# Gathers of the score stage: a wait for V's first half before each group's first gather

## The reference

```python
h = jnp.maximum(_layernorm(x, axis=-1), 0.0)
Q, K, V = ((h @ W).reshape(n, H, D) for W in (Wq, Wk, Wv))      # H = 8 heads of D = 32
scores = jnp.einsum('ehd,ehd->eh', Q[dst], K[src]) * SCALE
# softmax of the scores over the edges of one dst, w
msg = V[src] * w[:, :, None]
out = jnp.zeros((n, H, D), msg.dtype).at[dst].add(msg)
# then: output projection, residual, layer norm, feed-forward with gelu, residual, layer norm
```

## Time and profile before

| what | value |
|---|---|
| median of three runs (lowest to highest) | 1763.69 us (1762.94 to 1768.16) |
| the profiled execution | 1771.17 us |
| its span, first to last instruction | 1769.3 us |
| busy: PE, DVE, ACT, POOL | 93%, 86%, 75%, 72% of the span |
| score stage | from the start to about 402 us |

### The profile page before, as it was taken

The page is one execution under the profiler, slowest core; times in us unless marked ns, Lnnn a source line. Parts: engine busy times, 40 slices in busy tenths (PEclk is TensorE's granted clock), DMA queues, the critical chain, the costliest instruction groups (busy, mean ns, idle before and its releaser), DMA issues.

```text
span 1769.3 us, 31077 instructions
## 1 busy us (share of the span) xinstructions
PE 1642.7 (93%) x10389; PEld 1472.7 (83%) x10389; DVE 1512.9 (86%) x4615; ACT 1320.0 (75%) x2419; POOL 1270.5 (72%) x1281
## 2 busy tenths in 40 slices
PE   2878888799888999999999999999999999999997
PEld 2767777687666899999999999999999999999997
DVE  1566666778773899999999999999999999999997
ACT  1465556565444888888888888888888888888884
POOL 7364545505666788888888888888888888888883
PEclk7798889999988999999999999999999999999999
DMA  5487637713425577777777777777777777777761
GB/s 173 142 311 269 239 131 274 288 37 127 133 100 125 123 171 179 176 170 177 177 171 176 175 174 176 175 175 172 176 176 174 174 178 172 175 178 172 174 138 66
DMA packets 95280, 303.91 MB, mean 172 GB/s; under 512 B 16236, under 2 KB 21834, under 8 KB 95120
## 3 DMA queue, kind: packets, MB, share of 16 engines
q0 software_dynamic: 42336, 138.54, 38.9%
q1 hardware_dynamic: 52784, 163.38, 26.5%
HBM read 134.61 MB, written 118.53 MB: 143 GB/s over the span
## 4 chain that ended last, share of the span: by engine, by line
PE 84%; issue 6%; DVE 4%; ACT 3%; another core or an unknown queue 2%; DMA 0%; DVEq 0%; SPq 0%; POOLq 0%; POOL 0%; ACTq 0%
PE banks L962 32%; PE banks L951 30%; PE banks L384 8%; PE banks L937 5%; PE banks L406 3%; PE banks L904 2%; PE banks L392 2%; ACT a_hs L335 2%; DVE c_total L811 1%; PE banks L923 1%; PE banks L376 1%; DVE c_msg L799 1%; ACT a_htd_hi L302 1%; PE banks L893 0%
## 5 line engine op out<-in xcount | busy, mean ns | idle before, releaser
L962 PE MATMUL banks<-d_w_hi,d_act_hi 128*128 128x256 f32 x1564 | 457.4, 292 | 0.0
L962 PE MATMUL banks<-d_w_lo,d_act_hi 128*128 128x256 f32 x1564 | 442.0, 283 | 0.0
L962 PE MATMUL banks<-d_w_hi,d_act_lo 128*128 128x256 f32 x1564 | 441.6, 282 | 0.0
L1159 ACT ACTIVATE vt<-vt,d_zx_nmr,d_zx_rstd 128x256 f32<-128x256 f32 x391 | 222.8, 594 | 141.6 <-POOL d_zx_nmr L1278 141.6
L951 PE MATMUL banks<-d_zt_hi,d_w_hi 128*128 128x512 f32 (+1 forms) x784 | 306.8, 391 | 2.2 <-DVE d_zt_lo L1044 2.2
L951 PE MATMUL banks<-d_zt_lo,d_w_hi 128*128 128x512 f32 (+1 forms) x784 | 306.4, 391 | 0.0
L951 PE MATMUL banks<-d_zt_hi,d_w_lo 128*128 128x512 f32 (+1 forms) x784 | 305.4, 390 | 0.0
L962 PEld LDWEIGHTS banks<-d_w_hi,d_act_lo 128*128 128x128 f32 x1564 | 298.9, 191 | 0.0
L962 PEld LDWEIGHTS banks<-d_w_hi,d_act_hi 128*128 128x128 f32 x1564 | 298.5, 191 | 0.0
L962 PEld LDWEIGHTS banks<-d_w_lo,d_act_hi 128*128 128x128 f32 x1564 | 297.9, 190 | 0.0
L1260 POOL TENSOR_TENSOR vt<-vt,d_g_row 128x1024 f32<-128x1024 f32 x98 | 289.3, 2952 | 2.9 <-ACT vt L1159 2.9
(11 more groups left out here) (167 smaller groups left out, 3629.4 us busy)
## 6 DMA issues: line engine op xcount, KB each, us to landing
agg_scratch<-vt SPq DMA_DIRECT2D x100, 512.0 KB
vt<-in_x SPq DMA_DIRECT2D x97, 512.0 KB
vt<-agg_scratch POOLq DMA_DIRECT2D x97, 512.0 KB, 5.5
vt<-vt POOLq DMA_DIRECT2D x97, 512.0 KB, 7.5
out<-vt SPq DMA_DIRECT2D x97, 512.0 KB, 2.9
a_xd<-in_x,a_idx POOLq DMA_INDIRECT x98
a_xs<-in_x,a_idx POOLq DMA_INDIRECT x98
score_scratch<-a_score SPq DMA_DIRECT2D x98, 4.0 KB
```

Source lines behind the costliest of these rows:

```text
L962: ins = nc.tensor.matmul(Y[s % 2][:, j, :], a[:, c, j * P:(j + 1) * P], w[:, c, :], start=False, stop=(c == KF - 1 and w is w2_lo), skip_g ...
L1159: ins = nc.scalar.activation(zn[gz % 2][:, j, :], z[gz % ZR][:, j, :], ACT.Identity, bias=zx_nmr[:, at % NR, 0, j:j + 1], scale=zx_rstd[:, ...
```

## The change

GpSimd waits once more before the first gather of each group from group 4 on, for the first half of V of step g - 4:

```diff
@@ -166,6 +166,8 @@
                         continue
                     if g >= XG and j == 0:
                         pool.wait_ge(h_done[side], g + 1 - XG)
+                    if g >= XG + 1 and n == 0:
+                        pool.wait_ge(v_done, KD * (g - XG - 1) + 1)
                     at = g * 2 * GT + n
                     nc.gpsimd.indirect_dma_start(
                         xg[side][g % XG][:, j, :], None, x, bass.IndirectOffsetOnAxis(idx[:, at:at + 1], 0),
```

## The result

The changed kernel took 1799.45 us (median of five runs, 1798.23 to 1804.04) against 1763.69 us of the kernel before (now over five runs, 1758.46 to 1768.16): a ratio of 1.0208, 95% interval 1.0182 to 1.0234. It is slower by 35.8 us in the medians; the forecast was +38. The profiled execution took 1799.45 us with a span of 1797.6 us, 28.3 us more than the span in the profile before.

The account below looks back on a forecast made before the run. Gather bursts hold back TensorE's completions in the score stage; one burst of eight over Q and K makes steps 16.8 us, so 20 x (16.8 - 14.91) = +38, 1763.7 + 38 = 1802 us; own range 1768 to 1820, 8-in-10 range 1731 to 1822.

Parts of the forecast that it names:

- Lateness of data: nothing.: Gathered rows read by VectorE: starting the gathers later exposes no latency, so the sum has no term for it.
- some 14 us are left for landing: Time for the last destination gather's rows to land before VectorE's statistics read them, with a step of at least 10.97 us.
- The burst's place: Each step's eight gathers run from x = 0.1 to 9.8, over Q and K; release comes at x = 11.8.
- x: Time in us within a step's cycle, counted from the end of V's first half of step g - 4.
- 33 matmuls go out.: Under the burst, TensorE issues 33 closely spaced matmuls from Q's start at x = 2.7, then crawls from x = 6.6.
- the first rival: Hold begins around the fifth or sixth gather, so Q completes before it: 13.25 us a step, -33 us, 1731 us; 25%.
- the 3 us of the earlier trace: Step 6: recorded end of h_s transposes to ScalarE's start, taken to agree with TensorE's reported end being an estimate.
- After the release: 3.4 us at the full clock, 5.5 at the half.: TensorE's work from the release to the end of V's first half; a step is thus 15.2 or 17.3 us.
- third of K: Part of K's 24 matmuls left after the release, 0.9 us at the full clock.
- The clock falls in three steps of four.: TensorE's granted clock drops during the 5.2 us crawl in three of four steps, giving 16.8 us a step.
- Bytes: Rival: the holds are gathers contending with the fills on shared DMA engines, giving no difference; left inside the 10%.
- That the stalls aren't the profiler's doing.: Score stage: 79 us of stalls against only 7.5 us between the profiled execution and the median of runs.

Follow-up runs that it names:

- r1: The changed kernel itself, nothing altered, run on a second chip beside the kernel before: 1650.16 us against 1648.96 us, ratio 1.0005.
- k2: Changed kernel with the added wait on the whole of K instead of V's first half, seventh chip: 1749.0 us against 1765.83 us for the kernel before (0.9901).
- l1: Changed kernel with the added wait one step later, on V's first half of step g - 3: 1685.53 us against 1649.2 us for the kernel before (1.0225).
- s1: Changed kernel with the added wait on K's first half instead of V's, fourth chip: 1745.58 us against 1765.17 us for the kernel before (0.9894).
- k1: Changed kernel with the added wait on the whole of K instead of V's first half, sixth chip: 1649.49 us against 1648.63 us for the kernel before (0.9999).
- s2: Changed kernel with the wait on all of K and 120 warm-up matmuls of 512 columns, not 70 of 256: 1765.54 us against the kernel before's 1765.45 (1.0012).

## Why the prediction was right, point by point

**The sign and the size**: +38 us forecast, +35.8 measured in the medians, and the mechanism was the one named: one burst of eight in each step, K under it, TensorE crawling, the copy of K late, the clock at its half level. This is shown, by the rows of the cycle above, by r1, in which the hold is missing and the loss with it, and by k2, which moves the burst and nothing else and gets the time back (on another chip with the hold). The sum itself was +38 for twenty steps, and held to that it is 12 us too high: the steps of the two profiles give 324.10 - 298.21 = +25.9. In a profile I had forecast 1809 us and it took 1799.45. The medians came nearer because the profiled execution that I took 14.91 us a step from was 7.5 us above its median.

**Lateness of data: nothing.** Right for this change. My "some 14 us are left for landing" was too generous, as l1 shows: with one step of 11 us taken from it, 3 us should have been left over, and VectorE already waits up to 6.2 us. One step later the delay costs 2.2% even without the hold.

**The burst's place.** I had the first gather at x = 0.1 and the last one's end at 9.8; GpSimd starts only 0.77 us after V's first half, in every step, and the end is at 10.5. The release at +2.0 us was right. Together 12.46 instead of 11.8 us: 0.7 us too little, from costing the path from TensorE through the semaphore to GpSimd at nearly nothing. The earlier trace rows could not show it, since before the gathers waited for ScalarE; it is a step I did not bound.

**"33 matmuls go out."** Wrong. In the changed kernel 39 to 46 of the 48 go out closely spaced (median 43), and the last of these starts at x = 7.5 (median), not 6.6. The argument behind it, that in step 8 the hold was there from Q's start, falls too. The hold begins some 5 us into a burst; in step 8 the burst began at 162.44 and Q at 167.41, so the two moments were the same by chance of place. That start after the fourth or fifth gather was the first rival's mechanism, which I had at 25%. It was right in its premise and did not win, because K's first half ends, closely spaced, at about x = 7.1, after the hold's start at 5.9, so its copy waits for the release all the same. And the 3 us of the earlier trace rows, which I gave as agreeing with TensorE's end being an estimate, are no error of the estimate: in the traces without the hold the recorded end of the transposes and the start of their copy are 0.04 us apart whenever ScalarE is idle.

**After the release: 3.4 us at the full clock, 5.5 at the half.** Over 17 steps (2 to 10 and 13 to 20; step 11's burst is broken by a pause) measured 1.6 us in the one at the full clock, and 3.3 to 5.3 in the others, median 4.1. As nearly all of K had gone out, the "third of K" that I had put behind the release was not there. This term was 1.4 us too large a step.

**The clock falls in three steps of four.** In 16 of these 17 it was at 0.50 for the whole (seven times) or a part of the stretch after the release. So it fell more often than forecast, and with less left for it to slow.

The errors cancel in part: +0.7 for the hold, -1.4 for the rest of the step, +0.4 for the clock, and some -0.3 because steps 1 and 12 were shorter than the seventeen; 16.2 us a step stands against 16.8. That the medians came within 2.2 us of the forecast is therefore luck in two ways: errors that cancel, and a base profile 7.5 us above its median. The step of my working to mend is the second: I read one instance, step 8, where a table of all bursts would have shown from when on completions are late.

**Bytes.** The rival falls. Step 11 and step 20 of the changed kernel have no fills and move 85 and 64 GB/s, and take 16.9 and 16.8 us, no less than their neighbours at 250. (Step 12, the third without fills, took 13.0; GpSimd's burst of step 11 had paused 1.89 us after its first gather, and the two steps together are 29.8 us, a little less than any two neighbours without step 12, 31.0 and more.) And where there is no hold, 390 GB/s do no harm. A changed kernel with the fills cut to a few bytes (f1) was to test this directly and gave no result, so no run with the hold is wholly without fills.

**"That the stalls aren't the profiler's doing."** This argument was empty. I compared a profiled time with the times of runs, and by the span and the clock that stand beside every timed run, these were observed as well. The number of records of semaphore updates in the traces differs in a way that I would have liked to know then, for one and the same program:

```
records of semaphore updates in the trace: whole run, and to the end of the score stage
before, prediction's chip (hold)     15167    2736
changed, prediction's chip (hold)    15809    3273
s1, fourth chip (hold)               15283    2822
k2, seventh chip (hold)              15449    2839
changed, second chip (no hold)       21295    7014
k1, sixth chip (no hold)             21301    7013
```

The instructions are recorded in full in all of them. In the traces with the hold 53 to 61% of the updates of the score stage have no record, when one takes the count of those without it as full. That is also why ScalarE's late copies are put down to "remote" in the rows. It may be that whatever carries those records is congested on some chips by the gathers' own updates, and that TensorE's completions wait behind it. The Trainium skill (NOTIFIC — the notification-queue block, Overflow: three behaviours, one of which stalls the engine) says that the block that writes such records does one of three things when a ring of it is full: it drops the new record, overwrites the oldest, or stalls the engine that produces them. Missing records by themselves would fit the first two, and no run here shows that an engine is stalled this way: I had no way to run the kernel unobserved, and records can be missing for the same cause that delays the completions, without being the cause. It stays open, and with it whether the 35.8 us exist in an execution that nobody records.

No variant was made for bursts of at most four gathers with a pause between them. By what the pairs above show they would end before the hold begins, and step 6 of the kernel before, with a burst of four under Q, took the 10.97 us of its own work. s1 shows something of the pause, since in six of its steps the source gathers waited for their slot and the eight fell into four and four. The transposes of h_s ended 0.88 us into the second four each time. After pauses of 0.79, 0.94 and 1.41 us their copy was 2.34, 0.70 and 3.67 us late, after pauses of 1.22, 1.28 and 1.75 us only 0.04 us. (In the third case ScalarE itself was busy for 0.65 of the 3.67 us.) So a pause of 1.4 us isn't safe, and all pauses of 1.5 to 2.5 us in s1 and the kernel before were followed by transposes on time in the first 1.5 us of the next burst.

## What to carry to other kernels

When a forecast rests on a stall that the trace puts down to nothing (idle by "issue" or "remote"), measure first how the stall depends on where in the burst the victim stands, over all of its instances; one scatter over the trace before would have given the 5 us and with it the better place for the wait. Cost the path of a new wait as well as the work behind it: 0.8 us from a matmul's end to the first gather closed a ring of three links in every step. And run the unchanged kernel on another chip before explaining a loss: a 2.1% effect that is 0.05% on the next chip belongs to where it was measured as much as to the kernel, and a version should be chosen that is safe in both (here the gathers behind the whole of K: 0.990 and 1.000).

## What the runs showed of the hardware

- The same program takes 1649 us in four sets of measurements and 1764 to 1766 us in four others, 7% apart, with nothing in between. In all traces of the second kind TensorE's completions reach ScalarE late beside long runs of indirect gathers (by up to 6.0 us), in all of the first kind never (0.04 us after the recorded end of the transposes).
- Where it exists, the hold of a burst begins about 5 us after its first gather (the fourth has ended at 4.7) and ends mostly 1.7 to 2.1 us after its last (in the changed kernel once 1.3).
- TensorE goes on issuing for a while under the hold and then at one matmul per 0.7 to 2.8 us. How far it gets is not one number: some 33 matmuls from the hold's start in step 8 of the kernel before and about 30 in k2, but only about 16 in the changed kernel (x = 5.9 to 8.0, one in 0.12 us). What is counted there is open. The matmuls of the crawl mostly start about 0.7, 1.4, 2.1 or 2.8 us apart, multiples of 0.70 us (201.39 - 200.67 = 0.72, 200.67 - 199.25 = 1.42; in s2 28.56 - 26.45 = 2.11).
- While it crawls the granted clock falls to 0.50 (1.2 of 2.4 GHz) and stays there beyond the release, 4.7 us in the cycle shown, so a stall of 4.5 us made the next 4.7 us of work run at half speed.
